# Local attention on eight cores: the per-row softmax offset becomes one bias per query tile, and one reload of the gated rows is issued earlier

## The chip, the cores and the metric

The kernel runs on the 8 NeuronCores of one Trainium2 chip, without any exchange between them. Each core handles 2048 of the 16384 tokens. The time is the device time of the slowest core, in microseconds (us). In the profile PE is TensorE, PEld its weight loads, DVE is VectorE, ACT is ScalarE, POOL is GpSimd and SP is SyncE; SPq rows are DMA instructions issued from SP's queue. PEclk is the granted TensorE clock, where 1.00 is 2.4 GHz and 0.50 is 1.2 GHz.

## The reference

One layer: a layer norm, then the sum of the input, an attention branch with its own feed-forward, and a second feed-forward branch. The attention looks back over 44 fixed offsets:

```python
xn = _rmsnorm(x, norm1_scale)
q, k, v = split(xn @ w_qkv)                      # 16 heads of 64
scores = einsum('bhnd,bhnod->bhno', q, k[src]) * scale + pos_bias.T
scores = where(t < offset, -inf, scores)
alpha = softmax(scores)
out = einsum('bhno,bhnod->bhnd', alpha, v[src])
gate = sigmoid(xn @ w_gate + b_gate)
x = x + out * gate @ w_out
x = x + silu(rms(x) @ w_ffn_gate) * (rms(x) @ w_ffn_up) @ w_ffn_down
```

A softmax does not change when the same number is subtracted from all scores of a row, so any offset that keeps the exponentials in range will do.

## The kernel before

Everything is ordered by hand. Each engine has one list of instructions, and `emit` puts every wait of an instruction in front of it as an instruction of its own. The helper `V` makes each VectorE instruction wait for the one before it (`vC`), and `SE` does the same on ScalarE (`sC`). `DA` issues a DMA from SP, `DW` one from POOL. `barrier()` makes all engines wait for everything, DMAs too.

The stages are: the norms (to some 368 us in the trace), the projections for K, Q, the gate and V (to 790), the attention (820 to 1583), the output projection (1585 to 1870), the branch's feed-forward (to 2453), and the second feed-forward (line 993, to the end).

The attention runs over 16 query tiles `qt` of 128 tokens, and in each over 16 heads `h`. `NJ` is 8: eight key tiles of 128 hold all the keys that a query tile may need. For a head:

- `p2_passB` (lines 626 to 670): TensorE fills `p_B`, two PSUM banks of scores with the keys on the partitions and the queries along the row. First come two matmuls of one row of ones with `s_nb4` (line 635), which write minus the offset of each query, 1x512 each. Then come eight matmuls of K with Q (line 644). ScalarE takes the exponential in two halves (line 655) and VectorE multiplies each half by the table `s_MT` (line 662).
- `p2_av` (lines 672 to 700): eight matmuls with V (line 684), then three small VectorE instructions, copy, reciprocal and the product with the gate (lines 693, 696, 698). It is emitted one head late, behind the `p2_passB` of the next head.

The offsets of the next tile are made inside the current one. After `p2_passB` of head 0, `p2_tile_loads` loads the next Q and gate tiles. After heads 1 to 4, `p2_passA_grp` makes sample scores of four heads each (line 594) and VectorE takes their maxima by query (line 604). After head 5, `p2_passA_tail` (line 611) negates them (line 613), and three DMAs from SP, each waiting for the one before, transpose them (616), store them (618) and load them as a row (620). Only the `p2_passB` of the next tile waits for the third (`qNB`). For tile 0 all this runs before the loop.

At a tile's end its gated output is stored to `d_gated` (line 722). After a barrier the output projection runs over 4 blocks of 4 tiles: SP first issues 144 small DMAs with constants (lines 762 to 769), then for each block the reload of `d_gated` to `s_g4` (line 779) and of the normed input to `xnb33` (line 784). TensorE transposes `s_g4` in 32 pieces (line 793), each copied by VectorE (797), then makes eight output groups (807), each added to `xnb33` by VectorE (813) before its PSUM buffer, one of two, is free again. Line 823 is VectorE's next step behind the last of these adds. The weight `wo` comes on POOL's queue (line 771).

Of the kernel before, what the change touches and what calls it, by code (L numbers as in the profile page):

```python
# [8 lines left out]
F32 = mybir.dt.float32  # L9
BF16 = mybir.dt.bfloat16  # L10
# [5 lines left out]
D = 1024  # L16
# [67 lines left out]
def build_nc(offsets, tap=None, upto=99, p2sub=99):  # L84
# [303 lines left out]
    if upto == 0:  # L388
# [140 lines left out]
    for h in range(H):  # L529
# [12 lines left out]
    s_nb = [sb("s_nb0", [128, 16], BF16, st2), sb("s_nb1", [128, 16], BF16, st2)]  # L542
    s_nbT = [sb("s_nbT0", [16, 128], BF16, st2), sb("s_nbT1", [16, 128], BF16, st2)]
    s_nb4 = [sb("s_nb40", [65, H * 128], BF16, st2), sb("s_nb41", [65, H * 128], BF16, st2)]
    s_E = [sb("s_E0", [128, NJ * 128], BF16, st2), sb("s_E1", [128, NJ * 128], BF16, st2)]
    s_at = [sb("s_at0", [128, NJ * 128], BF16, st2), sb("s_at1", [128, NJ * 128], BF16, st2)]
    s_rd = sb("s_rd", [128, 1], F32, st2)
# [13 lines left out]
        "pb_ms": {},  # L561
        "qld": [0, 0],
        "gld": [0, 0],
        "nb4": [0, 0],
        "gd_store": [0, 0],
        "pA_guard": 0,
        "av_free": [0, 0],
# [175 lines left out]
    s_g4 = sb("s_g4", [128, 4 * D], BF16, st3b)  # L743
    g43 = s_g4[:, :].rearrange("p (n d) -> p n d", n=4)
# [30 lines left out]
    prev_r1_store = 0  # L775
    sr_evac_v = 0
    ti = 0
    for blk in range(4):
        DA(qG4, lambda s, blk=blk: s.dma_start(
            g43[:, :, :],  # L780
            d_gated.ap().rearrange("n p d -> p n d")[:, blk * 4:(blk + 1) * 4, :]),
           waits=[(tM, tM.n)])
        g4q = qG4.n
# [360 lines left out]
```

How the kernel before makes its waits and increments, by code:

```python
    def emit(self, eng, fn, incs=(), waits=()):  # L54
        lst = self.q[eng]
        for (c, v) in waits:
            if v > 0:
                lst.append(lambda e, _h=c.h, _v=v: e.wait_ge(_h, _v))
        ivals = []
        for (c, k) in incs:
            c.n += k
            ivals.append((c.h, k))
        def run(e, _fn=fn, _iv=tuple(ivals)):
            inst = _fn(e)
            for (_h, _k) in _iv:
                inst = inst.then_inc(_h, _k)
        lst.append(run)
# [2 lines left out]
def _finish(nc, P, dma_sems):  # L72
    for c_ in dma_sems.values():
        if c_.n > 0:
            P.emit("sync", lambda s, _h=c_.h, _v=c_.n: s.wait_ge(_h, _v))
    with nc.Block() as blk:
        blk.tensor(lambda t: [f(t) for f in P.q["tensor"]])
        blk.vector(lambda v: [f(v) for f in P.q["vector"]])
        blk.scalar(lambda s: [f(s) for f in P.q["scalar"]])
        blk.gpsimd(lambda g: [f(g) for f in P.q["gpsimd"]])
        blk.sync(lambda s: [f(s) for f in P.q["sync"]])
# [2 lines left out]
def build_nc(offsets, tap=None, upto=99, p2sub=99):  # L84
# [105 lines left out]
    def barrier():  # L190
        vals = [(tM, tM.n), (vC, vC.n), (sC, sC.n)]
        vals += [(c, c.n) for c in _dma_sems.values()]
        for eng in ("tensor", "vector", "scalar", "gpsimd", "sync"):
            for (c, v) in vals:
                if v > 0:
                    P.emit(eng, lambda e, _h=c.h, _v=v: e.wait_ge(_h, _v))
# [812 lines left out]
           waits=[(tM, tM.n)])  # L1009
        xhq = qXH.n
        P.q["tensor"].append(lambda t, _v=xhq: t.wait_ge(qXH.h, _v))
```

## Time and profile before

| what | us |
|---|---|
| median of 2 runs | 5026.72 |
| the two runs | 4989.46 and 5063.99 |
| the profiled execution, its own time | 4994.68 |
| its span, slowest core (core 1) | 4993.1 |
| spans of the 8 cores | 4965.5 to 4993.1 |
| PE busy (share of the span) | 4115.5 (82%) |
| DVE busy | 1068.8 (21%) |
| ACT busy | 617.2 (12%) |
| line 635, the matmuls with ones, busy | 263.3 |

The busy shares are means over stages that differ. In the attention, 749 us of the span, PE is busy 680 us and DVE 444 us, at a granted clock of 0.50. Busy time leaves out what an engine's queue spends on wait instructions between two operations; that is to be read from the timeline.

### The profile page before, as it was taken

What the parts mean: (1) busy time and instruction counts of PE and PEld (TensorE: products, weight loads), DVE (VectorE), ACT (ScalarE), POOL (GpSimd) and SP (SyncE); (2) the same over time, 40 slices, a digit from 0 to 9 for tenths busy, and PEclk for the clock granted to TensorE, in tenths of its full rate; (3) what the DMA queues carried; (4) which work ended last, traced back from release to release, by engine and by line L of the source; (5) the groups of instructions that cost most, each with busy time, mean ns of one, the idle gap of its engine ahead of it and who ended that gap; (6) DMA issues with size and microseconds to landing.
All of it is one profiled execution on the core that took longest, in us unless ns stands there. A gap on an engine that the chain in (4) does not pass through costs nothing.

```text
span 4993.1 us, 54328 instructions; the slowest of 8 cores (4965.5 to 4993.1 us)
## 1 busy us (share of the span) xinstructions
PE 4115.5 (82%) x20226; PEld 1878.4 (38%) x20226; DVE 1068.8 (21%) x2261; ACT 617.2 (12%) x802; POOL 194.0 (4%) x159
## 2 busy tenths in 40 slices
PE   1228776899896457696898999999989899999999
PEld 0003333444443113342343444444434344444444
DVE  1762234555554340030012000000010200000001
ACT  0000001444342001100020000000002000000000
POOL 0000000000000000000010000000001100000000
PEclk8558986555555668898999999999999999999999
DMA  7421221000001122204466656565676756656667
GB/s 140 101 71 22 68 43 44 21 21 15 21 19 25 51 84 47 47 1 105 114 75 82 83 70 84 68 83 69 85 152 76 93 68 75 78 74 79 75 77 144
DMA packets 486884, 343.15 MB, mean 69 GB/s; under 512 B 55603, under 2 KB 448820, under 8 KB 484580
## 3 DMA queue, kind: packets, MB, share of 16 engines
q0 software_dynamic: 384176, 219.69, 34.3%
q1 hardware_dynamic: 102452, 119.98, 8.1%
q8 instruction: 169, 2.77, 0.2%
q14 instruction: 87, 0.71, 0.0%
HBM read 513.56 MB, written 53.61 MB: 114 GB/s over the span
## 4 chain that ended last, share of the span: by engine, by line
PE 72%; DMA 10%; DVE 9%; issue 3%; SPq 2%; ACT 2%; DVEq 1%; another core or an unknown queue 1%; ACTq 0%; POOLq 0%
PE p L993 47%; PE p_f L927 3%; PE p_gm L428 3%; PE p_f L877 3%; PE p_f L896 3%; PE p_B L635 3%; PE p_B L644 3%; PE p_gm L490 2%; PE p_av L684 2%; DVE s_at L662 2%; PE p_o L807 1%; DMA s_hs<-w3T 1%; DMA s_hs<-h1T 1%; DMA s_w<-wqkv 1%; DVE s_xa L366 1%
## 5 line engine op out<-in xcount | busy, mean ns | idle before, releaser
L993 PE MATMUL p<-s_hb,s_hs 128*128 128x512 bf16 x6144 | 1335.0, 380 | 45.5 <-DMA s_hs<-w1T 18.7
L993 PE MATMUL p<-s_ha,s_hs 128*128 128x512 bf16 x5120 | 1110.5, 380 | 45.7 <-DMA s_hs<-h1T 38.3
L993 PEld LDWEIGHTS p<-s_hb,s_hs 128*128 128x128 bf16 x6144 | 600.8, 98 | 779.7 <-issue 67.0
L993 PEld LDWEIGHTS p<-s_ha,s_hs 128*128 128x128 bf16 x5120 | 501.6, 98 | 654.6 <-issue 54.5
L1051 DVE SCALAR_TENSOR_TENSOR s_oo<-p,s_s,s_rr 128x1024 f32<-128x1024 f32 x16 | 20.5, 1283 | 2004.3 <-PE p L993 1919.5
L655 ACT ACTIVATE s_E<-p_B 128x512 bf16<-128x512 f32 x512 | 305.7, 597 | 436.9 <-PE p_B L644 315.7
L644 PEld LDWEIGHTS p_B<-s_qt,s_K 64*128 64x128 bf16 x2048 | 195.9, 136 | 214.1 <-issue 214.1
L635 PE MATMUL p_B<-s_nb,s_onesb 1*128 1x512 bf16 x512 | 263.3, 615 | 7.4 <-DMA s_nb<-d_nb 7.4
L644 PE MATMUL p_B<-s_qt,s_K 64*128 64x128 bf16 x2048 | 263.7, 306 | 0.0
L662 DVE TENSOR_TENSOR s_at<-s_E,s_MT 128x512 bf16<-128x512 bf16 x512 | 217.6, 425 | 188.2 <-ACT s_E L655 86.0
L428 PE MATMUL p_gm<-s_xa,s_w 128*128 128x512 bf16 x704 | 161.2, 393 | 64.8 <-DMA s_w<-wqkv 64.7
L684 PE MATMUL p_av<-s_V,s_at 128*128 128x65 bf16 x2048 | 168.0, 242 | 30.6 <-DVE s_at L662 29.3
L877 PE MATMUL p_f<-s_xn,s_wga 128*128 128x512 bf16 x704 | 153.8, 382 | 45.9 <-DMA s_wga<-wfg 45.9
L927 PE MATMUL p_f<-s_hatt,s_wd 128*128 128x512 bf16 x704 | 154.6, 383 | 42.2 <-DMA s_wd<-wfd 42.2
L896 PE MATMUL p_f<-s_xn,s_wga 128*128 128x512 bf16 x704 | 153.4, 381 | 38.1 <-DMA s_wga<-wfu 38.1
L1031 ACT ACTIVATE s_ha<-p,s_sh 128x1024 bf16<-128x1024 f32 x64 | 71.3, 1114 | 815.8 <-PE p L993 815.8
L347 PE MATMUL p_b<-s_row,s_onesf 1*128 1x512 f32 x14 | 14.3, 1122 | 190.9 <-DVE s_row L345 190.9
L1020 DVE SCALAR_TENSOR_TENSOR s_ha<-p,s_s,s_ha 128x1024 bf16<-128x1024 f32 x64 | 82.1, 1284 | 408.8 <-PE p L993 408.8
L1031 ACT ACTIVATE s_hb<-p,s_sh 128x1024 bf16<-128x1024 f32 x64 | 71.3, 1114 | 784.8 <-PE p L993 784.8
L684 PEld LDWEIGHTS p_av<-s_V,s_at 128*128 128x128 bf16 x2048 | 119.5, 125 | 101.9 <-issue 100.0
L1014 ACT ACTIVATE s_ha<-p,s_s 128x1024 bf16<-128x1024 f32 x64 | 71.3, 1114 | 554.9 <-PE p L993 554.9
L793 PE MATMUL p_t<-s_id,s_g 128*128 128x128 bf16 x128 | 33.3, 265 | 122.5 <-DMA s_g<-d_gated 105.3
(104 smaller groups left out, 1870.2 us busy)
## 6 DMA issues: line engine op xcount, KB each, us to landing
s_hs<-h1T POOLq DMA_DIRECT2D x32, 2048.0 KB, 19.2
s_hs<-h2T POOLq DMA_DIRECT2D x32, 2048.0 KB, 19.0
s_hs<-w1T POOLq DMA_DIRECT2D x32, 512.0 KB, 5.7
s_hs<-w2T POOLq DMA_DIRECT2D x32, 512.0 KB, 5.8
s_hs<-w3T POOLq DMA_DIRECT2D x8, 2048.0 KB, 19.4
s_x<-xT SPq DMA_DIRECT2D x7, 2048.0 KB, 11.9
d_grep<-d_gtab SPq DMA_DIRECT2D x16, 512.0 KB, 34.7
d_r<-s_r SPq DMA_DIRECT2D x4, 2048.0 KB, 6.9
```

Of the source, the lines that this page charges most:

```text
L428: T(lambda t, oc4=oc4, kc=kc, b0=b0, b=b, p=p: t.matmul(p[:, b * 512:(b + 1) * 512], w83[:, kc, oc4 * 128:(oc4 + 1) * 128], xa3[:, kc, (b0 ...
L490: T(lambda t, tt=tt, kc=kc, p=p: t.matmul(p[:, 0:512], xa3[:, kc, tt * 128:(tt + 1) * 128], w83[:, kc, :], start=(kc == 0), stop=(kc == 7) ...
L635: T(lambda t, h=h, bk=bk, pB=pB, r0=r0, bi=bi: t.matmul(pB[:, bk * 512:(bk + 1) * 512].rearrange("p (r q) -> p r q", r=4), s_onesb[r0:r0 + ...
L644: T(lambda t, jj=jj, ktile=ktile, g=g, r0=r0, pB=pB, q3=q3: t.matmul(pB[:, jj * 128:(jj + 1) * 128], K3[r0:r0 + 64, g, ktile * 128:(ktile ...
L655: SE(lambda s, pB=pB, par=par, hx=hx, HW2=HW2: s.activation(s_E[par][:, hx * HW2:(hx + 1) * HW2], pB[:, hx * HW2:(hx + 1) * HW2], AF.Exp), ...
L662: V(lambda v, h=h, par=par, hx=hx, HW2=HW2: v.tensor_tensor(s_at[par][:, hx * HW2:(hx + 1) * HW2], s_E[par][:, hx * HW2:(hx + 1) * HW2], M ...
L684: T(lambda t, jj=jj, ktile=ktile, h=h, pav=pav: t.matmul(pav[:, 0:65], s_at[par][:, jj * 128:(jj + 1) * 128], V4[:, ktile, h, :], start=(j ...
L877: T(lambda t, oc=oc, kc=kc, b=b, pf=pf: t.matmul(pf[:, b * 512:(b + 1) * 512], wga3[:, kc, oc * 128:(oc + 1) * 128], xn23[:, kc, b * 512:( ...
L896: T(lambda t, oc=oc, kc=kc, b=b, pf=pf: t.matmul(pf[:, b * 512:(b + 1) * 512], wga3[:, kc, oc * 128:(oc + 1) * 128], xn23[:, kc, b * 512:( ...
L927: T(lambda t, oc=oc, kc=kc, b=b, pf=pf: t.matmul(pf[:, b * 512:(b + 1) * 512], wd3[:, kc, oc * 128:(oc + 1) * 128], ha3[:, kc, b * 512:(b ...
L993: T(lambda t, o2=o2, kc=kc, b=b, pp=pp, src3=src3, sl3=sl3, n_kc=n_kc: t.matmul(pp[:, b * 512:(b + 1) * 512], sl3[:, kc, o2 * 128:(o2 + 1) ...
L1031: SE(lambda s, oc=oc, pp=pp: s.activation(dst3[:, oc, :], pp[:, :], AF.Gelu, scale=ssc[:, oc:oc + 1]), waits=[(tM, fm)])
```

## The change

The offset is no longer one number for each query and head but one for the whole query tile. `p2_passA_tail` now takes the largest of the 16 maxima of each query on VectorE, negates it, transposes the column with the same DMA, takes the minimum of that row of 128 on VectorE, spreads the single number over the 128 partitions with one matmul of one column, and copies it to `s_negB`. The second and third DMA are gone. The exponential takes `s_negB` as its bias operand and waits for it. The two matmuls with ones and the wait for `qNB` are gone from `p2_passB`; the first matmul in each PSUM bank now has `start`.

The space `s_g4` is allocated before the attention, and the reload of the first four gated tiles is issued from SP behind the store of tile 3, waiting for both store queues. Block 0 of the output projection takes it from there. The wait lists of its first transpose and of the reload of `xnb33` name a few more semaphores.

```diff
     def p2_passA_tail(qt):
         bi = qt & 1
-        V(lambda v, bi=bi: v.tensor_scalar_mul(s_nbp[:, 0:16], s_b[bi][:, :], -1.0),
+        V(lambda v, bi=bi: v.tensor_reduce(s_bq[:, :], s_b[bi][:, :], axis=AX.X, op=ALU.max),
           waits=[(qNB[bi ^ 1], qNB[bi ^ 1].n)])
+        V(lambda v: v.tensor_scalar_mul(s_nbp[:, 0:1], s_bq[:, :], -1.0))
         nb_ms = vC.n
         DA(qNB[bi], lambda s: s.dma_start(s_nbTp[:, :], s_nbp[:, :], transpose=True),
            waits=[(vC, nb_ms)])
-        DA(qNB[bi], lambda s, bi=bi: s.dma_start(d_nb.ap()[bi], s_nbTp[0:16, :]),
-           waits=[(qNB[bi], qNB[bi].n)])
-        DA(qNB[bi], lambda s, bi=bi: s.dma_start(
-            bass.AP(s_nb4[bi], 0, [[64 * H * 128, 2], [128, H], [1, 128]]),
-            bass.AP(d_nb, bi * H * 128, [[0, 2], [128, H], [1, 128]])),
-           waits=[(qNB[bi], qNB[bi].n)])
-        st_p2["nb4"][bi] = qNB[bi].n
+        nbq = qNB[bi].n
+        V(lambda v, nbq=nbq: v.tensor_reduce(
+            s_nbm[:, :], s_nbTp[0:1, :], axis=AX.X, op=ALU.min),
+          waits=[(qNB[bi], nbq)])
+        nbm_v = vC.n
+        T(lambda t: t.matmul(p_A[0][:, 0:1], s_onesb[0:1, :], s_nbm[:, :],
+                             start=True, stop=True, tile_position=(0, 0)),
+          incs=[(tM, 1)],
+          waits=[(vC, max(nbm_v, st_p2["pA_guard"]))])
+        nbb_ms = tM.n
+        V(lambda v, bi=bi, nbb_ms=nbb_ms: v.tensor_copy(s_negB[bi][:, :], p_A[0][:, 0:1]),
+          waits=[(tM, nbb_ms), (sC, sC.n)])
+        st_p2["negb_v"][bi] = vC.n
+        st_p2["pA_guard"] = vC.n
@@ p2_passB
-        fw = [(sC, st_p2["exp_done"][par]), (qNB[bi], st_p2["nb4"][bi])] + \
+        fw = [(sC, st_p2["exp_done"][par])] + \
              ([(qQT[bi], st_p2["qld"][bi])] if h == 0 else [])
-        for bk in range(NJ // 4):
-            T(lambda t, h=h, bk=bk, pB=pB, r0=r0, bi=bi: t.matmul(
-                pB[:, bk * 512:(bk + 1) * 512].rearrange("p (r q) -> p r q", r=4),
-                s_onesb[r0:r0 + 1, :],
-                s_nb4[bi][r0:r0 + 1, h * 128:(h + 1) * 128].unsqueeze(1).broadcast_to((1, 4, 128)),
-                start=True, stop=False,
-                tile_position=(r0, 0)),
-              waits=fw if bk == 0 else ())
...
-                start=False, stop=(jj % 4 == 3),
+                start=(jj % (NJ // 2) == 0), stop=(jj % 4 == 3),
...
-                s_E[par][:, hx * HW2:(hx + 1) * HW2], pB[:, hx * HW2:(hx + 1) * HW2], AF.Exp),
+                s_E[par][:, hx * HW2:(hx + 1) * HW2], pB[:, hx * HW2:(hx + 1) * HW2], AF.Exp,
+                bias=s_negB[bi][:, :]),
                waits=[(tM, st_p2["pb_ms"][h])] +
-                     ([(vC, st_p2["mask_done"][par])] if hx == 0 else []))
+                     ([(vC, max(st_p2["mask_done"][par], st_p2["negb_v"][bi]))] if hx == 0
+                      else [(vC, st_p2["negb_v"][bi])]))
@@ the loop over tiles
         st_p2["gd_store"][bi] = qGD[bi].n
+        if qt == 3:
+            DA(qG4, lambda s: s.dma_start(
+                g43[:, :, :], d_gated.ap().rearrange("n p d -> p n d")[:, 0:4, :]),
+               waits=[(qGD[0], st_p2["gd_store"][0]), (qGD[1], st_p2["gd_store"][1])])
+            p3_pre["g4q0"] = qG4.n
@@ the loop over blocks
+        if blk == 0:
+            g4q = p3_pre["g4q0"]
+        else:
+            DA(qG4, lambda s, blk=blk: s.dma_start(
+                g43[:, :, :],
+                d_gated.ap().rearrange("n p d -> p n d")[:, blk * 4:(blk + 1) * 4, :]),
+               waits=[(tM, tM.n)])
+            g4q = qG4.n
```

## Rows read from the trace of the kernel before

**Rows 1.** Groups by line: shapes, count | busy us, mean ns | idle before.
```profile
L635 PE MATMUL p_B<-s_nb,s_onesb 1*128 1x512 bf16 x512 | 263.3, 615 | 7.4 <-DMA s_nb<-d_nb 7.4
L334 ACT ACTIVATE s_row<-s_row,s_cv 1x512 f32<-1x512 f32 x7 | 5.0, 720 | 260.9 <-DVE s_row L332 260.9
L341 ACT ACTIVATE s_row<-s_row 1x512 f32<-1x512 f32 x7 | 4.4, 629 | 32.0 <-DVE s_row L339 32.0
```

**Rows 2.** Busy by stretch, attention: busy PE, PEld, DVE, ACT, POOL; PEclk, DMA, GB/s.
```profile
834.00:1583.00 749.00, 680.08 (x4848) 358.07 (x4848) 443.75 (x1415) 306.99 (x513) 0.00 (x0) 0.50 0.07 18
```

**Rows 3.** Timeline, a head above 5: start, us, engine line operation [idle before <-releaser].
```profile
908.22 1.03 PE L635 MATMUL p_B<-s_nb,s_onesb 1*128 1x512 bf16 x2
909.11 0.43 DVE L662 TENSOR_TENSOR s_at<-s_E,s_MT 128x512 bf16<-128x512 bf16 x1 [0.31 <-DVE s_gd L698]
909.18 1.03 PE L644 MATMUL p_B<-s_qt,s_K 64*128 64x128 bf16 x8
909.77 0.42 DVE L662 TENSOR_TENSOR s_at<-s_E,s_MT 128x512 bf16<-128x512 bf16 x1 [0.24 <-DVE s_at L662]
...
910.36 1.34 ACT L655 ACTIVATE s_E<-p_B 128x512 bf16<-128x512 f32 x2 [1.14 <-PE p_B L644]
910.37 0.23 DVE L693 COPY s_avs<-p_av 128x65 f32<-128x65 f32 x1 [0.17 <-PE p_B L644]
...
910.70 1.03 PE L635 MATMUL p_B<-s_nb,s_onesb 1*128 1x512 bf16 x2
...
910.97 0.28 DVE L698 SCALAR_TENSOR_TENSOR s_gd<-s_avs,s_rd,s_gtt 128x64 bf16<-128x64 f32 x1
911.56 0.43 DVE L662 TENSOR_TENSOR s_at<-s_E,s_MT 128x512 bf16<-128x512 bf16 x1 [0.31 <-DVE s_gd L698]
```

**Rows 4.** Timeline, the added VectorE work of a head from 1 to 4.
```profile
895.49 0.95 DVE L604 TENSOR_REDUCE s_b<-p_A 128x2 f32<-128x256 f32 x2 [0.17 <-DVE s_at L662]
```

**Rows 5.** Timeline, the tail behind head 5.
```profile
902.65 0.17 DVE L613 TENSOR_SCALAR s_nbp<-s_b 128x16 bf16<-128x16 f32 x1 [0.17 <-DVE s_at L662]
902.90 1.10 SPq L616 DMA_TRANSPOSE s_nbTp<-s_nbp  x1
...
904.19 0.42 DVE L662 TENSOR_TENSOR s_at<-s_E,s_MT 128x512 bf16<-128x512 bf16 x1 [0.31 <-DVE s_gd L698]
...
905.23 0.32 SPq L618 DMA_DIRECT2D d_nb<-s_nbTp  x1
```

**Rows 6.** Timeline, before the first tile.
```profile
822.99 0.95 DVE L604 TENSOR_REDUCE s_b<-p_A 128x2 f32<-128x256 f32 x2 [0.99 <-PE p_A L594]
...
830.54 0.33 SPq L618 DMA_DIRECT2D d_nb<-s_nbTp  x1
...
834.19 1.01 PE L635 MATMUL p_B<-s_nb,s_onesb 1*128 1x512 bf16 x2 [7.43 <-DMA s_nb<-d_nb]
```

**Rows 7.** Timeline, from one tile to the next.
```profile
883.59 0.38 SPq L573 DMA_DIRECT2D s_qt<-d_q  x1
...
886.54 0.63 PE L594 MATMUL p_A<-s_K,s_qt 64*128 64x128 bf16 x4 [1.19 <-DMA s_qt<-d_q]
...
887.62 0.42 DVE L604 TENSOR_REDUCE s_b<-p_A 128x2 f32<-128x256 f32 x1 [0.17 <-DVE s_at L662]
```

**Rows 8.** Timeline, block 0 of the output projection.
```profile
1659.35 0.38 SPq L779 DMA_DIRECT2D s_g<-d_gated  x1
...
1666.07 0.37 PE L793 MATMUL p_t<-s_id,s_g 128*128 128x128 bf16 x2 [84.73 <-DMA s_g<-d_gated]
...
1679.32 15.88 PE L807 MATMUL p_o<-s_gT,s_wo 128*128 128x512 bf16 x64 [0.63 <-DVE s_gT L797]
...
1696.17 2.29 DVE L823 CAST s_r1b<-s_r 128x4096 bf16<-128x4096 f32 x1
```

**Rows 9.** DMA issues: count, KB each, median us from issue to landing.
```profile
s_xnb<-d_xn SPq DMA_DIRECT2D x4, 1024.0 KB, 5.3
...
s_wo<-wout POOLq DMA_DIRECT2D x1, 2048.0 KB, 16.3
```

More of the change, by code:

```diff
@@ L392, in build_nc @@
         return nc
+    st3pre = ExitStack()
+    s_g4 = sb("s_g4", [128, 4 * D], BF16, st3pre)
+    g43 = s_g4[:, :].rearrange("p (n d) -> p n d", n=4)
     st_kv = ExitStack()
@@ L541, in build_nc @@
     s_b = [sb("s_b0", [128, 16], F32, st2), sb("s_b1", [128, 16], F32, st2)]
-    s_nb = [sb("s_nb0", [128, 16], BF16, st2), sb("s_nb1", [128, 16], BF16, st2)]
-    s_nbT = [sb("s_nbT0", [16, 128], BF16, st2), sb("s_nbT1", [16, 128], BF16, st2)]
-    s_nb4 = [sb("s_nb40", [65, H * 128], BF16, st2), sb("s_nb41", [65, H * 128], BF16, st2)]
+    s_bq = sb("s_bq", [128, 1], F32, st2)
+    s_nbm = sb("s_nbm", [1, 1], BF16, st2)
+    s_negB = [sb("s_negB0", [128, 1], F32, st2), sb("s_negB1", [128, 1], F32, st2)]
     s_E = [sb("s_E0", [128, NJ * 128], BF16, st2), sb("s_E1", [128, NJ * 128], BF16, st2)]
@@ L563, in build_nc @@
         "gld": [0, 0],
-        "nb4": [0, 0],
+        "negb_v": [0, 0],
         "gd_store": [0, 0],
@@ L647, in p2_passB @@
                 q3[r0:r0 + 64, g, :],
-                start=False, stop=(jj % 4 == 3),
+                start=(jj % (NJ // 2) == 0), stop=(jj % 4 == 3),
                 tile_position=(r0, 0)),
-              incs=[(tM, 1)] if jj == NJ - 1 else ())
+              incs=[(tM, 1)] if jj == NJ - 1 else (),
+              waits=fw if jj == 0 else ())
         st_p2["pb_ms"][h] = tM.n
@@ L654, in p2_passB @@
         for hx in range(2):
-            SE(lambda s, pB=pB, par=par, hx=hx, HW2=HW2: s.activation(
-                s_E[par][:, hx * HW2:(hx + 1) * HW2], pB[:, hx * HW2:(hx + 1) * HW2], AF.Exp),
+            SE(lambda s, pB=pB, par=par, hx=hx, HW2=HW2, bi=bi: s.activation(
+                s_E[par][:, hx * HW2:(hx + 1) * HW2], pB[:, hx * HW2:(hx + 1) * HW2], AF.Exp,
+                bias=s_negB[bi][:, :]),
                waits=[(tM, st_p2["pb_ms"][h])] +
-                     ([(vC, st_p2["mask_done"][par])] if hx == 0 else []))
+                     ([(vC, max(st_p2["mask_done"][par], st_p2["negb_v"][bi]))] if hx == 0
+                      else [(vC, st_p2["negb_v"][bi])]))
             e_ms = sC.n
@@ L702, in build_nc @@
     V(lambda v: v.memset(s_nbp[:, :], 0.0))
+    qG4 = DS("qG4")
+    p3_pre = {"g4q0": 0}
     p2_tile_loads(0)
@@ L742, in build_nc @@
     wo3 = s_wo[:, :].rearrange("p (k o) -> p k o", k=8)
-    s_g4 = sb("s_g4", [128, 4 * D], BF16, st3b)
-    g43 = s_g4[:, :].rearrange("p (n d) -> p n d", n=4)
     s_gT = sb("s_gT", [128, 8 * 512], BF16, st3b)
@@ L756, in build_nc @@
     p_bc3 = ps("p_bc3", [128, 512], F32, st3b)
-    qG4 = DS("qG4")
     qXN3 = DS("qXN3")
@@ L777, in build_nc @@
     ti = 0
+    p2_end_v = vC.n
+    p2_end_s = sC.n
     for blk in range(4):
[L779 to L783, printed above, removed]
+        if blk == 0:
[6 more added lines that the diff above has]
+            g4q = qG4.n
         DA(qXN3, lambda s, blk=blk: s.dma_start(
@@ L786, in build_nc @@
             xn_w[:, :, HALO + blk * 512: HALO + (blk + 1) * 512]),
-           waits=[(vC, vC.n)])
+           waits=[(vC, vC.n), (qXN[0], p0["xnst"][0]), (qXN[1], p0["xnst"][1])])
         xnq = qXN3.n
@@ L792, in build_nc @@
                 fw = [(vC, pt_free[ti])] + ([(qG4, g4q)] if (ttl == 0 and c == 0) else [])
+                if blk == 0 and ttl == 0 and c == 0:
+                    fw += [(vC, p2_end_v), (sC, p2_end_s)]
                 T(lambda t, ttl=ttl, c=c, pt=pt: t.transpose(
@@ L852, in build_nc @@
         st3.close()
+        st3pre.close()
         ctx.close()
@@ L943, in build_nc @@
     st3.close()
+    st3pre.close()
     if upto == 4:
```

## The prediction

> **What bounds the kernel now.** I read four views in this order. The groups by line tell what the removed work weighs: 512 matmuls with ones, 263.3 us busy on TensorE [rows 1]. The busy time by stretch tells where they lie: the attention takes 749 us, TensorE busy 680 of them at a granted clock of 0.50 (1.2 GHz) and VectorE 444 [rows 2]. By these two, TensorE looks like the bound and a third of its work goes. The timeline of one head says otherwise [rows 3]. VectorE's `s_at` starts at 909.11 and the next head's at 911.56: 2.45 us. It does 0.43 + 0.42 + 0.23 + 0.28 and a reciprocal inside the 0.37 between 910.60 and 910.97. Between them it stands still for 0.24, 0.17 and 0.31 us. These gaps do not follow what other engines do: the copy at 910.37 reads the output of matmuls long done, and its "releaser" on TensorE only happens to end then. They follow the number of wait instructions in front: two before the copy (0.17), three before the second half (0.24), four before the first half (0.31). So every VectorE instruction runs as soon as its own queue lets it, and 2.45 us is VectorE's queue, full. TensorE's period is 910.70 - 908.22 = 2.48, so both run neck and neck, with TensorE's results ready a little ahead. The exponential that starts at 910.36 has its first half ready at about 910.96, with some 0.24 of handing over 911.20, and is used at 911.56: 0.36 us of slack. In heads 1 to 4 VectorE also has the two maxima, 0.95 + 0.17 [rows 4], and is the bound alone, at 2.45 + 1.12 = 3.57 us a head.
>
> For the output projection the timeline shows TensorE idle for 84.73 us until the reload of `d_gated`, issued at 1659.35 behind the 144 small DMAs on SP [rows 8].
>
> **Part 1, the ones matmuls go.** From 908.22 to 909.18 they cost 0.96 us of TensorE a head, 246 us for 256 heads. What hides the gain is VectorE's own queue of 2.45 us, to which the edit does nothing. In steady heads the slack grows from 0.36 to 1.3 us and the period stays: gain 0. Were that cover gone (VectorE's waits merged), it would be worth up to 0.96 a head. Only where VectorE waits for a chain is there something: between tiles. There the next step is the load of Q, issued at 883.59 once the store has gone out; its first use is at 886.54 and the maxima start at 887.62, held by VectorE [rows 7]. With the scores of heads 0 and 1 some 0.96 and 1.9 us earlier, VectorE is ready first, and the maxima start when their matmuls end: 886.54 + 0.63 + 0.12 = 887.29. The load is late next, and it does not move. Gain 0.33 us, 15 times: -5.0.
>
> **Part 2, the new tail.** This is the main term. Before, nothing in the tile waits for the three DMAs. Now VectorE itself waits for the transpose and TensorE for VectorE, both in order. Behind VectorE's wait stand copy, reciprocal and product of head 4 and the masks of heads 6 and later; behind TensorE's stand the V matmuls of head 4, the scores of head 6, and so ScalarE too. By the clock of [rows 5]:
>
> - 902.65: maximum of 16, taken as 0.17 (the 128x16 instruction there); gap 0.10; negation 0.16: ends 903.08 instead of 902.82.
> - SP issues after 0.08, and 905.23 - 902.90 = 2.33 later the transpose has landed: 905.49.
> - minimum of 128 in one row: the trace has none. Below, 0.16 (a product of a few elements here takes 0.17); above, 0.43 for 256 elements out of PSUM, half of the 0.95 of two [rows 4]. It is nearer to the small one: 0.20, to 905.69.
> - VectorE to TensorE and back took 0.99 with four 128-column matmuls [rows 6]. Less the four (0.62 by the same matmuls [rows 7]) that is 0.18 each way. The one matmul takes about 0.12 of the queue: the V matmuls of head 4 start at 905.99.
> - They take 2.48 - 0.96 - 0.96 = 0.56: the scores of head 6 start at 906.55, and from scores to exponential it is 910.36 - 909.18 = 1.18: 907.73.
> - two exponentials 1.34, and each gets a pointer operand: line 334 with one takes 720 ns, line 341 without 629, so +0.09 each [rows 1]; the second half has a third wait, +0.07; handing over 0.17. The second mask of head 6 starts at 909.49. ScalarE at 1.6 us a head stays below 2.45.
>
> Before, that mask started at 904.19 + 0.66 = 904.85. So each tail costs 4.64 us. After it TensorE, with 1.5 us a head, regains its lead, but VectorE is full and gives nothing back. Bounds: 4.0, if only the first half decides and all small terms are at their low end, to 5.6, with 0.43 for the minimum and half a microsecond more on the restart. 15 tails: +69.6 (60 to 84).
>
> Before tile 0 the tail gets shorter. Scores started 834.19 + 0.96 = 835.15; now 830.54 + 0.26 (first reduction) + 0.30 (minimum) + 0.30 = 831.40 [rows 6]. With the slower exponentials: -3.5.
>
> **Part 3, the early reload.** Issued behind tile 3 on SP, it makes SP wait until that store has landed, and the Q load of tile 5 stands behind it. No row has this wait. The nearest small DMA is the transpose, 2.3 us, and the issue 0.4: at least 2.7. Above: that and the whole transfer of 1 MB ahead of the Q load, 1666.07 - 1659.35 = 6.7 [rows 8], 9.4. I take 5, between, since the two share the DMA engines: +5, once.
>
> In block 0 the 32 transposes (13.25 us) now run under the small DMAs, and so do the first two output groups: `wo` needs 16.3 us [rows 9] of more than 70. But the 84.73 us are not gained. The first add needs `xnb33`, still behind the 144 DMAs. It takes the slot at 1659.35, lands in 5.3 (1664.65; alone, by [rows 9]), and with two PSUM buffers TensorE has done two of eight groups. An add (0.7), and then six groups at (1696.17 - 1679.32) x 6/8 = 12.6: the step of line 823 comes at 1678 instead of 1696.17. With a landing as slow as that of the reload, 6.7, and a little restart: 1680. So -17 (-14 to -18).
>
> **Sum**: 69.6 - 5.0 - 3.5 + 5 - 17 = +49. The profiled execution took 4994.7 us, so 5044. That execution is near the lower of the two runs shown; the median, 5026.7, is 32 above it, and 5044 is 0.3% above the median. A few runs of this kernel can hardly tell less than 2% from no change.
>
> **Rivals.**
>
> *TensorE sets the pace after all* (other side): if VectorE's gaps are waits for TensorE, 11 heads of each of 16 tiles lose 0.96 us: -169, time 4875, 2.4% faster. For it: TensorE's 2.48 against 2.45, and 91% busy. Against it: the gaps are the same to 0.01 us in heads 1 to 4, where TensorE stands idle. It decides only if 0.85 us a head come off. The Trainium skill (VectorE: DVE Perf Modes, "The DRAIN you can't avoid") says that a semaphore after each instruction costs nothing extra; by that rule the gaps would not be the waits' own, which speaks for this rival. The trace disagrees with it, as the growth from 0.17 to 0.31 shows. Chance 5%.
>
> *The restart costs more than one head* (slower): if after the wait TensorE and VectorE run in lockstep for two more heads, each of them 2.45 us lost, a tail costs 9.5 and the sum is 5117, 2.4% slower. It decides from 8 us a tail. Against it: the chain from the end of a mask over V matmuls, scores and exponential to the mask two heads on is 0.1 + 0.56 + 1.18 + 0.7 + 0.24 = 2.8 us, and VectorE needs 3.8 for what lies between. Chance 10%, with one more head (5081) in the range.
>
> *The clock rises*: without the one-row matmuls TensorE could be granted 1.00 in the attention. Then the TensorE terms of a tail halve (0.12, 0.56 and 0.96 of 1.18): -0.8 each, -12, 5032. Against it: TensorE is busy 91% at 0.50 [rows 2] and gets less to do. The Trainium skill (TensorE: Matmul & The Clock Gate, "Why this matters for your kernels") says that keeping the engine continuously busy lifts it to full rate; by it the stage should already be at 1.00, and the row says no. Chance 5%.
>
> *The early reload does nothing for block 0*, if what comes behind the small DMAs decides it all: 5061. Chance 5%; the rest, 75%, is the forecast.
>
> **Numbers.** The forecast alone, with tails from 60 to 84, the reload and block 0 at their ends and 0.3% between runs: 5015 to 5080. The range goes from 5010 to 5105: the lower end holds the clock's case, the upper one the restart with one or nearly two heads, and a median that stands as high over its profile as that of the runs shown. Faster by over 2% is the first rival, 0.05; slower by over 2% the second and a little of the forecast's tail, 0.11; the rest 0.84.
>
> **What would show it.** VectorE's period in heads above 5 stays 2.45 with the same gaps, while TensorE shows idle time; one idle of about 2.4 us on VectorE before the minimum and one of about 6 us on TensorE, in each tile; tiles 51 instead of 749 / 16 = 46.8 us apart; exponentials at 0.69; the clock at 0.50; line 813 waiting for `xnb33` until about 1665 plus the attention's shift. It is wrong if the period falls below 2.4, or if tiles are under 49 or over 54 us apart.

## The result, and the profile after

| | before | after |
|---|---|---|
| median of all executions (their number) | 5059.3 us (10) | 5106.3 us (11) |
| lowest | 4986.3 | 5036.2 |
| profiled execution | 4994.7 | 5038.8 |
| its span | 4993.1 | 5037.2 |

The change makes the kernel slower by 1.0%: ratio 1.0099, 95% interval 1.0083 to 1.0115, which is under 2%. In about half of the executions of either kernel the cores of one die run at a lower mean granted clock and the execution takes 1 to 11% longer; the ratio leaves these out, the medians don't.

A group of the page of after (busy, mean ns | idle before, releaser), and the attention by stretch (columns as in [rows 2]):

```profile
L659 ACT ACTIVATE s_E<-p_B,s_negB 128x512 bf16<-128x512 f32 x512 | 351.8, 687 | 455.3 <-PE p_B L647 225.0
L690 PE MATMUL p_av<-s_V,s_at 128*128 128x65 bf16 x2048 | 181.5, 238 | 142.2 <-DVE s_at L668 140.9
```

```profile
827.00:1636.00 809.00, 448.72 (x4323) 323.39 (x4324) 448.35 (x1447) 350.77 (x510) 0.00 (x0) 0.50 0.07 18
```

TensorE's busy time falls from 680 us in a stretch of 749 to 449 in one of 809: the work was removed as the diff says, and the stage is 60 us longer. VectorE's busy time is the same, 444 and 448. The clock is 0.50 in both.

A head above 5 in the timeline of after, to be laid beside [rows 3]:

```profile
968.05 0.42 DVE L668 TENSOR_TENSOR s_at<-s_E,s_MT 128x512 bf16<-128x512 bf16 x1 [0.31 <-DVE s_gd L704]
...
968.72 0.42 DVE L668 TENSOR_TENSOR s_at<-s_E,s_MT 128x512 bf16<-128x512 bf16 x1 [0.24 <-DVE s_at L668]
968.73 0.38 PE L690 MATMUL p_av<-s_V,s_at 128*128 128x65 bf16 x4 [0.55 <-DVE s_at L668]
...
969.31 0.23 DVE L699 COPY s_avs<-p_av 128x65 f32<-128x65 f32 x1 [0.17 <-DVE s_at L668]
...
970.51 0.42 DVE L668 TENSOR_TENSOR s_at<-s_E,s_MT 128x512 bf16<-128x512 bf16 x1 [0.31 <-DVE s_gd L704]
```

VectorE's gaps of 0.31, 0.24 and 0.17 are those of before to 0.01 us, and its period is 2.46. What has changed is TensorE: it now waits 0.55 us for a mask in each head.

The tail, to be laid beside [rows 5]:

```profile
954.42 0.17 DVE L616 TENSOR_REDUCE s_bq<-s_b 128x1 f32<-128x16 f32 x1 [0.17 <-DVE s_at L668]
...
954.92 1.08 SPq L620 DMA_TRANSPOSE s_nbTp<-s_nbp  x1
957.23 0.28 DVE L623 TENSOR_REDUCE s_nbm<-s_nbTp 1x1 bf16<-1x128 bf16 x1 [2.38 <-DMA s_nbTp<-s_nbp]
...
957.66 0.16 PE L627 MATMUL p_A<-s_nbm,s_onesb 1*128 1x1 bf16 x1 [7.40 <-DVE s_nbm L623]
...
957.89 0.60 PE L690 MATMUL p_av<-s_V,s_at 128*128 128x65 bf16 x8
...
958.42 1.03 PE L647 MATMUL p_B<-s_qt,s_K 64*128 64x128 bf16 x8
...
959.60 0.69 ACT L659 ACTIVATE s_E<-p_B,s_negB 128x512 bf16<-128x512 f32 x1 [7.62 <-DVE s_gd L704]
...
961.35 0.42 DVE L668 TENSOR_TENSOR s_at<-s_E,s_MT 128x512 bf16<-128x512 bf16 x1 [0.40 <-ACT s_E L659]
```

Three engines stand still here, one behind the other: VectorE 2.38 us for the transpose, TensorE 7.40 in all until the minimum is there, ScalarE 7.62 until the next scores. From the first instruction of the tail to the second mask of head 6 (961.35) it is 6.93 us, where before it was 904.85 - 902.65 = 2.20.

The passage to the next tile, the one with the early reload, and block 0 (answering [rows 7] and [rows 8]):

```profile
935.56 0.39 SPq L576 DMA_DIRECT2D s_qt<-d_q  x1
...
939.42 0.95 DVE L607 TENSOR_REDUCE s_b<-p_A 128x2 f32<-128x256 f32 x2 [0.86 <-PE p_A L597]
...
1037.18 0.33 SPq L730 DMA_DIRECT2D d_gated<-s_gd  x1
1039.25 0.37 SPq L734 DMA_DIRECT2D s_g<-d_gated  x1
1039.71 0.46 SPq L576 DMA_DIRECT2D s_qt<-d_q  x1
...
1045.65 0.62 PE L597 MATMUL p_A<-s_K,s_qt 64*128 64x128 bf16 x4 [8.76 <-DMA s_qt<-d_q]
...
1663.25 5.23 PE L824 MATMUL p_o<-s_gT,s_wo 128*128 128x512 bf16 x16 [4.03 <-DMA s_wo<-wout]
...
1721.45 0.38 SPq L799 DMA_DIRECT2D s_xnb<-d_xn  x1
1726.73 0.69 DVE L830 TENSOR_TENSOR s_r<-p_o,s_xnb 128x512 f32<-128x512 f32 x1 [67.13 <-DMA s_xnb<-d_xn]
...
1727.57 12.40 PE L824 MATMUL p_o<-s_gT,s_wo 128*128 128x512 bf16 x48 [59.09 <-DVE s_r L830]
...
1740.94 2.29 DVE L840 CAST s_r1b<-s_r 128x4096 bf16<-128x4096 f32 x1
```

Usually the Q load goes out 0.4 us behind the store (here 935.15 and 935.56) and takes 2.95 us to its first use (883.59 to 886.54 in [rows 7]); behind tile 3 it goes out 2.5 us behind the store and takes 5.9 us. In block 0 TensorE's old idle of 84.73 us is gone, and a new one of 59.09 us has come in its place, behind the add that waits for the reload of `xnb33`.

The books, in us of the two profiled spans. "Tail to store" is from the issue of the transpose to the store of the tile, "store to tail" from there to the next transpose. The new reduction to one maximum puts the issue of the transpose off by 0.26 and so lies in "store to tail":

| where | before | after | difference | predicted |
|---|---|---|---|---|
| tail to store, mean of 15 | 26.99 | 31.54 | +4.55 each, +68 | |
| store to tail, mean without tile 3's, 14 passages | 20.0 | 19.5 | -0.5 each, -7 | |
| last tile | 41.4 | 40.5 | -0.9 | |
| these three together | | | +60 | +69.6 - 5.0 |
| first tile, from the issue of the transpose before it to that of the next | 27.96 | 24.75 | -3.2 | -3.5 |
| early reload, by which tile 3's passage exceeds the mean of the others | 0.5 | 5.0 | +4.5 | +5 |
| last store to the step of line 823 (now 840) | 113.17 | 97.52 | -15.7 | -17 |
| start of the kernel, and all behind block 0 | | | -1.7 | 0 |
| sum | 4993.1 | 5037.2 | +44.1 | +49 |

### The profile page after: what moved, and what is told of

Read it like the earlier page. It is cut to its first block, busy times and chain, and to the rows that moved or that the text cites. A ratio compares the mean times of both kernels' runs of the same rounds, so it can differ in the third digit from the quotient of the medians.

```text
span 5037.2 us, 53450 instructions; the slowest of 8 cores (5009.5 to 5037.2 us)
## 1 busy us (share of the span) xinstructions
PE 3890.9 (77%) x19730; PEld 1845.9 (37%) x19730; DVE 1078.2 (21%) x2309; ACT 663.3 (13%) x802; POOL 194.0 (4%) x159
## 4 chain that ended last, share of the span: by engine, by line
PE 67%; DVE 13%; DMA 10%; issue 5%; SPq 2%; ACT 2%; DVEq 1%; another core or an unknown queue 0%; ACTq 0%; POOLq 0%
PE p L1012 48%; DVE s_at L668 4%; PE p_gm L431 3%; PE p_f L895 3%; PE p_f L945 3%; PE p_f L914 3%; PE p_gm L493 2%; PE p_o L824 1%; DVEq L58 1%; DVE s_gd L704 1%; DMA s_hs<-h1T 1%; DMA s_w<-wqkv 1%; DVE s_avs L699 1%; DMA s_qt<-d_q 1%; ACT s_E L659 1%
## 5 line engine op out<-in xcount | busy, mean ns | idle before, releaser
L1070 DVE SCALAR_TENSOR_TENSOR s_oo<-p,s_s,s_rr 128x1024 f32<-128x1024 f32 x16 | 20.5, 1284 | 1997.6 <-PE p L1012 1893.2
L659 ACT ACTIVATE s_E<-p_B,s_negB 128x512 bf16<-128x512 f32 x512 | 351.8, 687 | 455.3 <-PE p_B L647 225.0
L690 PE MATMUL p_av<-s_V,s_at 128*128 128x65 bf16 x2048 | 181.5, 238 | 142.2 <-DVE s_at L668 140.9
L597 PE MATMUL p_A<-s_K,s_qt 64*128 64x128 bf16 x256 | 40.3, 399 | 145.0 <-DMA s_qt<-d_q 91.2
L431 PEld LDWEIGHTS p_gm<-s_xa,s_w 128*128 128x128 bf16 x704 | 70.4, 100 | 158.1 <-issue 81.9
```

Source lines behind the costliest of these rows:

```text
L431: T(lambda t, oc4=oc4, kc=kc, b0=b0, b=b, p=p: t.matmul(p[:, b * 512:(b + 1) * 512], w83[:, kc, oc4 * 128:(oc4 + 1) * 128], xa3[:, kc, (b0 ...
L659: SE(lambda s, pB=pB, par=par, hx=hx, HW2=HW2, bi=bi: s.activation(s_E[par][:, hx * HW2:(hx + 1) * HW2], pB[:, hx * HW2:(hx + 1) * HW2], A ...
L690: T(lambda t, jj=jj, ktile=ktile, h=h, pav=pav: t.matmul(pav[:, 0:65], s_at[par][:, jj * 128:(jj + 1) * 128], V4[:, ktile, h, :], start=(j ...
```

## Experiments

Ratios are to the kernel before, from runs on the same chip. Line numbers move by a few between kernels; the names stay.

**Do the ones matmuls pace anything?** The kernel before, with these two alone taken out:

```diff
@@ p2_passB, on before
-        for bk in range(NJ // 4):
-            T(lambda ...: t.matmul(pB[...], s_onesb[...], s_nb4[bi][...], start=True, stop=False))
...
-                start=False, stop=(jj % 4 == 3),
+                start=(jj % 4 == 0), stop=(jj % 4 == 3),
...
+              waits=fw if jj == 0 else ())            # the waits of the removed matmuls
```

> The kernel before without the two matmuls with ones of each head; nothing else is touched, the offsets are still made and waited for but no longer subtracted, so the softmax works without an offset. Theory, VectorE's queue sets the pace: the period of its masks in heads above 5 stays 2.45 us, TensorE shows some 0.5 us of idle time a head; only the passage from tile to tile and the rare late result gain, 0.3 to 0.8 us a tile, 5 to 15 us in all, ratio to before 0.997 to 0.999. Rival, TensorE sets the pace: 11 heads of 16 tiles lose 0.96 us each, 169 us, ratio 0.966, and the period falls to about 1.5 to 2.

Ratio 0.9965 (0.9945 to 0.9984). Timeline, a head above 5, and the attention by stretch:

```profile
908.37 0.43 DVE L655 TENSOR_TENSOR s_at<-s_E,s_MT 128x512 bf16<-128x512 bf16 x1 [0.31 <-DVE s_gd L691]
...
909.04 0.38 PE L677 MATMUL p_av<-s_V,s_at 128*128 128x65 bf16 x4 [0.56 <-DVE s_at L655]
...
910.82 0.43 DVE L655 TENSOR_TENSOR s_at<-s_E,s_MT 128x512 bf16<-128x512 bf16 x1 [0.31 <-DVE s_gd L691]
```

```profile
834.00:1583.00 749.00, 451.18 (x4320) 323.40 (x4320) 443.92 (x1414) 304.86 (x510) 0.88 (x1) 0.50 0.08 21
```

A third of TensorE's work goes, 680 us to 451 in the same stretch as [rows 2], and the head still takes 2.45. The rival in which TensorE sets the pace asked for 0.966. The small gain lies where VectorE waits for a chain: store to tail falls from 20.0 to 19.25, 15 times 0.75 = 11 us, of a total of about 17 (0.35% of 4990).

**What does a tail cost, the wait or the lost lead?** In after the minimum, the one-column matmul and the copy stand directly behind the transpose. First they are moved together, behind head 7, where the transpose has long landed; then one by one:

```diff
@@ the loop over tiles, on after; p2_passA_tail split in four
                 if h == 5:
                     p2_passA_tail(qt + 1)          # reduce, negate, transpose
+                if h == 7:
+                    p2_tail_red(qt + 1)            # minimum
+                if h == 8:                         # h == 7 in the first version
+                    p2_tail_mm(qt + 1)             # matmul
+                if h == 9:                         # h == 7 in the first version
+                    p2_tail_copy(qt + 1)           # copy to s_negB
```

All three behind head 7:

> The kernel after, with the tail split: maximum, negation and transpose stay behind head 5; minimum, matmul and copy stand together behind head 7, two heads or 4.9 us later, when the transpose (2.3 us) has long landed. Theory A, the cost of a tail is the wait for the transpose alone: a tail falls from 4.7 us to the added VectorE work of about 1 us, 56 us less in all, ratio to before 0.999. Theory B, TensorE loses its lead of a head as well, since its one matmul waits for a minimum that stands behind the masks of head 7: from the end of the mask 0.45 + 0.2 to the matmul, 0.56 V matmuls, 1.18 to the exponential, 1.76 to the second mask are 4.2 us, where 2.0 would do; a tail costs some 2.5 us, 33 us less than after, ratio 1.003.

The lowest of its four executions took 4999.7 us, beside some 4990 of before; there is no interval. Tail to store is 29.35 us (31.54 in after, 26.99 before): the tail still costs 2.4 us though nothing waits for the DMA.

```profile
955.81 0.28 DVE L627 TENSOR_REDUCE s_nbm<-s_nbTp 1x1 bf16<-1x128 bf16 x1 [0.17 <-DVE s_at L678]
956.24 0.16 PE L633 MATMUL p_A<-s_nbm,s_onesb 1*128 1x1 bf16 x1 [4.63 <-DVE s_nbm L627]
...
956.57 0.16 DVE L642 COPY s_negB<-p_A 128x1 f32<-128x1 f32 x1 [0.48 <-PE p_A L633]
...
959.11 0.42 DVE L678 TENSOR_TENSOR s_at<-s_E,s_MT 128x512 bf16<-128x512 bf16 x1 [1.05 <-ACT s_E L669]
```

The minimum starts 0.17 behind the mask, so it waits for no DMA, but TensorE still stands still for 4.63 us until the minimum is there, and VectorE's next mask waits 1.05 for ScalarE. Staggered:

> The kernel after, with the tail in four places: maximum, negation and transpose behind head 5, minimum behind head 7, the one matmul behind head 8, the copy behind head 9, so that neither engine waits for the other. Both theories: VectorE pays only its own three small instructions, 0.27 + 0.45 + 0.40 = 1.1 us a tile instead of 4.7, 54 us less than after, ratio to before 0.999; no idle time above 0.4 us on VectorE at these places. If the time stays near that of after, the tail was not the cause.

Ratio 0.9990 (0.9978 to 1.0001). Tail to store 27.94: the cost is 1.0 us, about what the minimum (0.28), the copy (0.16) and the gaps in front of them take on VectorE. TensorE's idle time before its one matmul is 1.56 us now:

```profile
951.58 0.28 DVE L627 TENSOR_REDUCE s_nbm<-s_nbTp 1x1 bf16<-1x128 bf16 x1 [0.17 <-DVE s_at L678]
...
952.00 0.16 PE L633 MATMUL p_A<-s_nbm,s_onesb 1*128 1x1 bf16 x1 [1.56 <-DVE s_nbm L627]
...
957.01 0.16 DVE L642 COPY s_negB<-p_A 128x1 f32<-128x1 f32 x1 [0.24 <-DVE s_at L678]
```

So of the 4.55 us of after 2.2 go when the minimum no longer waits for the DMA, 1.4 more when minimum, matmul and copy no longer stand in one head, and 1.0 is left for work.

**The early reload alone**, the second part of the change on the kernel before (the diff's parts around `s_g4`, `qt == 3` and `blk == 0`):

> The kernel before with only the early reload of the first four gated tiles. Theory: it costs 5 us behind tile 3, where SP waits for the store and the load of Q stands behind it, and gains 16 in block 0, which then waits for xnb33 behind the 144 small DMAs: 11 us less, ratio 0.998. Rival, the 84.7 us of idle time before block 0 go: ratio 0.984.

Ratio 0.998 (0.9935 to 1.0025). Both terms are there, whatever becomes of the tail: the tile behind tile 3 takes 52.6 us instead of 47.5, +5.1, and from the last store to the step of line 823 it is 96.5 instead of 113.17, -16.7.

**Do the gaps belong to the wait instructions?** The table `s_MT` is loaded once, but each mask waits for its semaphore. This wait goes from all masks but the first, and the one in after alike:

```diff
@@ p2_passB
-              waits=[(sC, e_ms), (qMT, mt_q)] +
+              waits=[(sC, e_ms)] + ([(qMT, mt_q)] if (qt == 0 and h == 0 and hx == 0) else []) +
```

On after:

> The kernel after, where VectorE waits for the table s_MT (semaphore qMT) once, at its first mask, and no longer before each mask. Theory, the gaps on VectorE are its own wait instructions at 0.07 us each and its queue sets the pace: the gaps of 0.31 and 0.24 before the masks become 0.24 and 0.17, the period of a head 2.45 becomes 2.31, 256 heads x 0.14 = 36 us less than after, ratio to before 1.003. Rival, the gaps are something else: ratio stays 1.010.

Ratio 1.0039 (1.0021 to 1.0057), from 1.0099. The timeline of VectorE:

```profile
966.36 0.42 DVE L668 TENSOR_TENSOR s_at<-s_E,s_MT 128x512 bf16<-128x512 bf16 x1 [0.24 <-DVE s_gd L704]
966.96 0.43 DVE L668 TENSOR_TENSOR s_at<-s_E,s_MT 128x512 bf16<-128x512 bf16 x1 [0.17 <-DVE s_at L668]
...
968.68 0.42 DVE L668 TENSOR_TENSOR s_at<-s_E,s_MT 128x512 bf16<-128x512 bf16 x1 [0.24 <-DVE s_gd L704]
```

A wait for a semaphore whose last DMA was issued some 155 us earlier (SP goes on to the Q load at 811.87 in this trace) costs 0.07 us: 0.31 becomes 0.24, 0.24 becomes 0.17, and the period 2.32. On before:

> The same edit in the kernel before: the wait for s_MT once. Here TensorE needs 2.48 us a head with its matmuls with ones, so in heads 6 to 15 nothing can be gained; in heads 1 to 5, where VectorE is the only bound, 0.14 us each: 16 x 5 x 0.14 = 11 us, ratio 0.998. If VectorE alone set the pace of the kernel before it would be 36 us, ratio 0.993; if it set none, 1.000.

Ratio 0.9968 (0.9955 to 0.9981). Half as much, since TensorE is right behind: VectorE runs at 2.32 for a few heads until it has used up TensorE's lead, and from then on at TensorE's 2.48 (masks at 917.06, 919.54 and 922.02 in this trace). The lines are from the passage between the two:

```profile
965.66 0.42 DVE L662 TENSOR_TENSOR s_at<-s_E,s_MT 128x512 bf16<-128x512 bf16 x1 [0.24 <-ACT s_E L655]
...
968.11 0.42 DVE L662 TENSOR_TENSOR s_at<-s_E,s_MT 128x512 bf16<-128x512 bf16 x1 [0.33 <-ACT s_E L655]
```

Here 0.33 is not the queue's own gap, which is 0.24 with these waits, but a result of ScalarE that comes late. Nearly the same number, 0.31 and 0.33, has two causes, and only the wait instructions in front of it tell which.

**Short waits behind the staggered tail.** Masks and the copy keep one wait each; the wait for VectorE's own last instruction goes too, where nothing of it is read:

```diff
@@ on the staggered version
+    def VN(fn, waits=()):                     # V without the wait for the instruction before
+        P.emit("vector", fn, incs=[(vC, 1)], waits=list(waits))
-            V(lambda v, ...: v.tensor_tensor(s_at ...), waits=[(sC, e_ms), (qMT, mt_q)] + ...)
+            VN(lambda v, ...: v.tensor_tensor(s_at ...), waits=[(sC, e_ms)])
-        V(lambda v, ...: v.tensor_copy(s_avs ...),
+        VN(lambda v, ...: v.tensor_copy(s_avs ...),
```

> The kernel after with the staggered tail (minimum, matmul and copy behind heads 7, 8 and 9), and VectorE's masks and its copy wait for one semaphore each (ScalarE's, TensorE's) instead of 3 or 4 and 2: the table is waited for once, the others are implied by earlier waits of the same queue or not needed. Theory: the three gaps of a head become 0.10 each, 0.42 us less a head, period 2.04; 256 x 0.42 = 107 us below the staggered tail's 0.999: ratio 0.978. If ScalarE (1.8 us a head) or the chain mask, V matmuls, scores, exponential (2.8 us against then 3.0) becomes the bound, less: down to half, ratio 0.988.

Ratio 0.9779, but with an interval from 0.9613 to 0.9945, too wide to place it. The trace shows tiles 37.7 us apart instead of the 47.4 of the staggered version, -9.7, where 0.42 x 16 = 6.7 were expected.

```profile
923.16 0.22 DVE L711 COPY s_avs<-p_av 128x65 f32<-128x65 f32 x1
...
923.48 0.16 DVE L714 RECIPROCAL s_rd<-s_avs 128x1 f32<-128x1 f32 x1
...
923.75 0.28 DVE L716 SCALAR_TENSOR_TENSOR s_gd<-s_avs,s_rd,s_gtt 128x64 bf16<-128x64 f32 x1
923.95 0.98 DVE L681 TENSOR_TENSOR s_at<-s_E,s_MT 128x512 bf16<-128x512 bf16 x2
```

The mask starts at 923.95, 0.20 behind the start of a product that lasts 0.28: the instructions overlap, which was not expected. No run takes the overlap apart from the shorter waits. VectorE is no longer the bound: in the last heads of this tile (core 1) the exponentials of two heads, 932.85 to 936.59, take 3.74 us, and ScalarE stands still only for 0.39 and three times 0.20 of it. That is 1.87 us a head, with ScalarE nearest to full.

**The same on before**, with the ones matmuls in place:

> The kernel before, where VectorE's masks and its copy of the V product wait for one semaphore each, as in the run of the kernel after that did so. TensorE still has its matmuls with ones, 2.48 us a head. Theory, in the kernel before TensorE's 2.48 stands right behind VectorE's 2.45, so taking VectorE's bound away shows the other: heads 6 to 15 stay at 2.48, heads 1 to 5 lose 0.6 each, 16 x 5 x 0.6 = 48 us, ratio 0.990. If the ones matmuls cost nothing even then, the gain would be the 3% that the same edit gave behind the staggered tail.

The lowest of four executions took 4958.3 us, some 31 less than before, where 48 were expected; there is no interval. TensorE, in the timeline:

```profile
907.07 1.03 PE L638 MATMUL p_B<-s_nb,s_onesb 1*128 1x512 bf16 x2
...
909.55 1.03 PE L638 MATMUL p_B<-s_nb,s_onesb 1*128 1x512 bf16 x2
```

2.48 us a head, TensorE's own work. The same edit takes 9.7 us off a tile behind the change and 2.0 here (47.0 to 45.0). So the ones matmuls cost 0.75 us a tile in before as it is, and some 8 (9.7 less 2.0) once VectorE's queue is short.

**The small DMAs.** The 144 loads of constants, ahead of the reload of `xnb33`, go out during the attention, ten behind head 9 of each tile:

```diff
@@ the loop over tiles
+            if h == 9:
+                consts(10)      # ten of the 144 DMAs; their old place is empty
```

On after:

> The kernel after, where the 144 small DMAs with constants are issued during the attention, ten behind head 9 of each tile, instead of ahead of block 0 of the output projection. Theory: xnb33 is then reloaded right behind the barrier, the output groups wait only for wo (16.6 us) and end at once; the step behind the last add of block 0 comes 34 us after the barrier instead of 95, 61 us less than after, ratio to before 0.998; the attention does not change, since SP has nothing else to issue behind head 9.

Ratio 0.9975 (0.9952 to 0.9998). Block 0 in its timeline:

```profile
1646.04 0.37 SPq L807 DMA_DIRECT2D s_xnb<-d_xn  x1
...
1664.51 15.52 PE L832 MATMUL p_o<-s_gT,s_wo 128*128 128x512 bf16 x64 [5.40 <-DMA s_wo<-wout]
...
1681.00 2.29 DVE L848 CAST s_r1b<-s_r 128x4096 bf16<-128x4096 f32 x1
```

The cast comes 60 us earlier than in after, and `wo` is the last thing waited for. On before:

> The kernel before, with the 144 small DMAs with constants issued during the attention, ten behind head 9 of each tile. Theory: the reload of the gated tiles is issued 2 us behind the barrier instead of 74 us later; 6.7 to land, 13.3 for the transposes, 16.9 for the output groups: the step behind the last add comes 74 us earlier, ratio 0.985. The early reload of the change would then have only the 6.7 us of landing left to hide.

Ratio 0.9836 (0.9767 to 0.9904): the largest gain of one edit to the kernel before, and it needs nothing of the change. From the last store to the step of line 823 it is 42.3 us instead of 113.17. With the spread alone on after it is 37.4, so once the queue is empty the early reload is worth 4.9 us in block 0, about what it costs behind tile 3.

**All together**: staggered tail, short waits, spread constants.

> The kernel after with the staggered tail, the short wait lists on VectorE and the 144 constants spread over the attention. If the parts add up: the staggered tail with short wait lists ran at about 4842 us where undisturbed, 59 less with the constants spread: 4783, ratio to before 0.959. ScalarE, 2.1 us a head, is then the bound of the heads above 5.

The lowest of four executions took 4774.9 us, about 0.957 of before; there is no interval. Since ScalarE is nearest to full, its waits were shortened as well:

```diff
@@ p2_passB, on the version above
+    def SN(fn, waits=()):
+        P.emit("scalar", fn, incs=[(sC, 1)], waits=list(waits))
-            SE(lambda s, ...: s.activation(s_E ...),
+            SN(lambda s, ...: s.activation(s_E ...),
-               waits=[(tM, st_p2["pb_ms"][h])] + ([(vC, max(...))] if hx == 0 else [(vC, negb_v)])
+               waits=[(tM, st_p2["pb_ms"][h]), (vC, max(...))] if hx == 0 else ()
```

> As the run with all three edits, and ScalarE's wait lists shortened too: the first exponential of a head waits for its scores and the mask (two semaphores instead of three), the second for nothing, since it follows the first in the same queue. Theory, ScalarE is the bound there: its gaps of 0.2 and 0.48 us become 0.1 or less and the head 1.6 us instead of 2.1 in heads above 5: 16 x 11 x 0.4 = 70 us less, 4713, ratio 0.945. TensorE's 1.55 us a head is right behind, so half of that is the lower bound of the gain.

Ratio 0.948 (0.9412 to 0.9548), the lowest 4736 us, the fastest of all. Tiles are 35.8 us apart.

```profile
924.58 1.26 ACT L675 ACTIVATE s_E<-p_B,s_negB 128x512 bf16<-128x512 f32 x2 [1.10 <-PE p_B L663]
...
926.10 1.26 ACT L675 ACTIVATE s_E<-p_B,s_negB 128x512 bf16<-128x512 f32 x2 [0.26 <-PE p_B L663]
```

Two exponentials take 1.26 us where they took 0.69 + 0.20 + 0.69 = 1.58. ScalarE stands still for 0.26 to 1.10 us before each pair now, so no engine is full; what the next bound is was not tried.

## Why the prediction was right, and where it was wrong

**The mechanism held.** "2.45 us is VectorE's queue, full": confirmed twice, by taking away TensorE's work alone (no change of the period) and by taking away a wait of VectorE (0.14 us less a head). The rival "TensorE sets the pace after all" falls with the first: 0.9965 instead of 0.966. It would come true only in a kernel whose waits have been thinned, as the pair of -2.0 and -9.7 us a tile shows. The Trainium skill (VectorE: DVE Perf Modes, "The DRAIN you can't avoid") says, of eight copies in a row, that a semaphore after each of them costs nothing extra. No run here repeats that, and for several waits in front of one instruction the runs show a cost: 0.07 us for the one that was taken away, and where the wait for the own predecessor is gone the next instruction starts before that one ends.

**The tail.** Predicted 4.64 us more from its first instruction to the second mask of head 6, measured 4.73 in the tail shown, and 4.81 in the mean (4.55 and the 0.26 of the added reduction). The steps: transpose 2.33 and 2.31; minimum 0.20 and 0.28; scores to exponential 1.18 and 1.18; exponential +0.09 and +0.09 (687 ns against 597, means of 512). TensorE's idle was put at about 6 us and is 7.40, which costs nothing further, since VectorE's wait is what all others hang on. The rival "the restart costs more than one head" is wrong: from the mask at 963.14 on, one head behind, the gaps are 0.31 and 0.24 as before.

**Passage to the next tile.** The term that was mis-sized: 0.33 us a tile, measured 0.76 (the 0.5 of the table and the 0.26 of the tail's added reduction, which lies in the same stretch), and 0.9 in the last tile; taking out the ones matmuls alone gave 0.75. I counted only that the first maximum starts earlier. What the rest is, the runs don't show. In the passage of [rows 7] the second maximum stands back for its matmuls (a gap of 0.46 where 0.11 is usual) and the first mask behind them by 0.59 where 0.31 is usual, and in after the pair of maxima takes 0.95 without a break (939.42). But the passages of one kernel differ, those of before from 19.7 to 20.5 us and the gain from 0.2 to 1.3, and in after the masks of a passage also wait up to 0.40 for the longer exponentials. All passages came to -11.7 us instead of -5.0. With +2.2 for the tails, +0.3 for the first tile, -0.5 for the reload, +1.3 for block 0 and -1.7 at the two ends of the kernel, this is the distance from +49 to +44.

**Early reload.** +5 by a bracket from 2.7 to 9.4, measured +5.1 alone and +4.5 in after. SP waited 1.7 us for the store and took 0.4 for the issue, and the Q load took 3.0 us longer to its first use. The size is right, but the middle of a wide bracket was luck rather than knowledge.

**Block 0.** Predicted -17 (-14 to -18), measured -15.7 in after and -16.7 alone. The add came when `xnb33` had landed, 5.3 us after its issue, as predicted. The rival "the early reload does nothing for block 0" is wrong by that amount, but the cause that it named, the queue of small DMAs, holds 60 us more in after, as the spread loads show.

**The clock.** 0.50 in the attention of every version, so the rival "the clock rises" falls. The Trainium skill (TensorE: Matmul & The Clock Gate, "Why this matters for your kernels") says that a continuously busy engine gets to full rate. In the last 900 us or so of before the trace agrees: from 4000 to 4900 TensorE is busy 897 of 900 us, at 1.00. In the attention it was busy 91% of 749 us before and 55% of 809 us after, at 0.50 both times. What keeps the clock down there, no run here tells.

**The step that failed is "Numbers".** The forecast, 5044 against a time of before of 4994.7, is a ratio of 1.0099, and that is what was measured; to the last digit this is luck, since the profiled spans differ by 44 us and not by 49. But the median of after is 5106.3 us and the range ended at 5105. For its upper end I let the median stand 32 us over the profile, as in the two runs shown. Two runs are not enough for that: of ten executions of before six are over 5050, and the medians stand 65 us (before) and 67 us (after) over their profiles. With 67 us instead of 32 the same working would have ended at 5140. Even that would have been luck in part: of the eleven executions of after five are at most 5048.4 us, the sixth and median is 5106.3 and the seventh 5304.6, so one execution more could have moved the median to 5077 or to 5205.

## What to carry to other kernels

An engine that is 60% busy can be the bound if its queue is full: lay two neighbouring periods side by side, and where the gaps between its instructions are the same in every head and grow with the number of wait instructions, count waits before you take work from the engine that looks busiest. A short chain put directly in the order of two queues costs its whole latency on both; let it start early and finish a few heads later, one step in each (4.55 us became 1.0). When one transfer is moved ahead of a crowded queue, ask what stands next behind the same crowd.

## What the runs showed of the hardware

- A VectorE instruction stands back 0.17, 0.24 or 0.31 us behind the one before it with two, three and four waits in front of it, though none of them holds it up; taking one away took 0.07 us off each gap.
- Without the wait for its own predecessor, a VectorE instruction starts before that one has ended: 0.20 us after the start of a product of 0.28 us. Two exponentials of 0.69 take 1.26 together. Short waits and this overlap together are worth 9.7 us a tile on VectorE, where 6.7 were worked out for the waits alone.
- The minimum over 128 values in one row took 0.28 us on VectorE, a matmul of one column 0.16 on TensorE.
- Small DMAs go out from SP about 0.5 us apart (1660.75, 1661.22, 1661.69 in after), and the 144 of them take from 1645.83 to the reload at 1721.45, 76 us. Moved under the attention they change the tiles' distance by less than 0.2 us.
